# Choosing the experts by pairs of token tiles, and three rows of a hand-written schedule changed

## The reference

```python
xn = layernorm(x)
# of the encoder layer
s    = sigmoid(einsum('bsd,hed->bhse', xn, Wsel))      # for values and for output
gate = s * (one of the two largest of 8, else 0)
v    = einsum('bsd,bhse,hedp->bhsp', xn, gate_v, Wv)
o    = softmax(rope(q) @ rope(k) / 8) @ v
src2 = einsum('bhsp,bhse,hepd->bsd', o, gate_o, Wo)
h    = LN(xn + src2);  ffn = LN(h + relu(h @ W1 + b1) @ W2 + b2)
out  = x + causal_attention(xn) + ffn
```

## Time and profile before

| | |
|---|---|
| median of 3 runs | 3388.97 us (3387.23 to 3390.75) |
| profiled execution | 3392.11 us, span 3390.0 us |
| PE, PEld busy | 3202.1 us (94%), 2398.4 us (71%) |
| DVE, ACT, POOL busy | 2454.9 us (72%), 2006.9 us (59%), 1574.4 us (46%) |
| granted clock of TensorE | 0.992 in the mean |
| DMA | 295.26 MB, mean 87 GB/s |

### The profile page before, as it was taken

How to read it: one execution, slowest core, us unless ns; L and a number is a source line. 1 busy time by engine, 2 the same in 40 slices (tenths; PEclk the granted TensorE clock), 3 DMA queues, 4 the chain that set the end, 5 groups by cost and what they waited for, 6 DMA issues and landing times.

```text
span 3390.0 us, 67613 instructions
## 1 busy us (share of the span) xinstructions
PE 3202.1 (94%) x19648; PEld 2398.4 (71%) x19648; DVE 2454.9 (72%) x4716; ACT 2006.9 (59%) x4637; POOL 1574.4 (46%) x1295
## 2 busy tenths in 40 slices
PE   1699999999999999999999999999999999997997
PEld 1577777777777777777777777777777777775886
DVE  6577777777777777777777777777777777775776
ACT  2456666666666666666666666666666666664443
POOL 4143355445444454335533554435544544445666
PEclk9899999999999999999999999999999999998999
DMA  5233333233333332333332332333323423324122
GB/s 165 68 80 87 86 97 87 66 87 97 89 84 80 90 100 71 85 85 98 84 82 74 101 96 70 87 92 94 84 73 79 110 76 85 87 60 127 63 81 75
DMA packets 116487, 295.26 MB, mean 87 GB/s; under 512 B 33888, under 2 KB 54624, under 8 KB 100064
## 3 DMA queue, kind: packets, MB, share of 16 engines
q1 hardware_dynamic: 116448, 294.78, 33.3%
HBM read 262.74 MB, written 31.98 MB: 87 GB/s over the span
## 4 chain that ended last, share of the span: by engine, by line
PE 71%; DVE 19%; issue 6%; ACT 1%; DMA 1%; POOL 1%; DVEq 0%; SPq 0%; POOLq 0%; ACTq 0%
PE bank L710 24%; PE bank L837 14%; PE bank L755 9%; PE bank L811 7%; PE bank L725 5%; DVE nmax L1208 4%; PE bank L782 2%; DVE vm L1229 2%; PE bank L730 2%; PE bank L823 2%; PE bank L953 2%; DVE vm L1272 2%; DVE uf L1311 2%; PE bank L791 2%; DVE vm L1254 1%
## 5 line engine op out<-in xcount | busy, mean ns | idle before, releaser
L579 POOL TENSOR_TENSOR u_l<-uf,u_h 128x512 fp32r<-128x512 f32 x512 | 688.9, 1356 | 717.5 <-ACT u_h L1101 717.4
L1208 DVE TENSOR_REDUCE nmax<-bank 128x1 f32<-128x512 f32 (+3 forms) x1024 | 552.8, 581 | 375.4 <-PE bank L725 369.5
L710 PE MATMUL bank<-wv_h,xx 128*128 128x512 f32 x2048 | 744.8, 410 | 12.0 <-DVE vm L1229 7.1
L1017 ACT ACTIVATE probs<-bank,nmax 128x512 f32<-128x512 f32 (+3 forms) x1024 | 591.4, 610 | 259.1 <-DVE nmax L1208 259.1
L1101 ACT ACTIVATE u_h<-uf 128x512 fp32r<-128x512 f32 x512 | 323.0, 631 | 657.4 <-DVE uf L1311 498.7
L710 PEld LDWEIGHTS bank<-wv_h,xx 128*128 128x128 f32 x2048 | 386.6, 189 | 193.1 <-issue 69.3
L575 POOL TENSOR_TENSOR v_sb<-v_next,zero_hb 128x512 f32<-128x512 f32 x64 | 74.6, 1166 | 893.8 <-PE bank L811 879.2
L837 PE MATMUL bank<-u_h,wo_h 128*128 128x512 f32 x1024 | 433.4, 423 | 34.3 <-issue 27.5
L755 PE MATMUL bank<-ident_sb,probs 128*128 128x128 f32 x3328 | 451.8, 274 | 2.3 <-ACT pt_e L1037 1.2
L755 PEld LDWEIGHTS bank<-ident_sb,probs 128*128 128x128 f32 x3328 | 387.4, 141 | 69.1 <-issue 13.5
L1311 DVE TENSOR_TENSOR uf<-oo,go 128x512 f32<-128x512 f32 x512 | 426.6, 843 | 10.1 <-POOL u_l L579 7.9
(11 more groups left out here) (167 smaller groups left out, 5595.5 us busy)
## 6 DMA issues: line engine op xcount, KB each, us to landing
go<-go_d SPq DMA_DIRECT2D x256, 512.0 KB, 6.6
xx<-xs_d SPq DMA_DIRECT2D x128, 512.0 KB, 5.0
oo<-scale_d SPq DMA_DIRECT2D x128, 128.0 KB, 2.9
a_d<-a_out SPq DMA_DIRECT2D x128, 128.0 KB, 2.3
pt_c<-in_x SPq DMA_DIRECT2D x16, 512.0 KB, 4.7
st<-in_wv SPq DMA_DIRECT2D x16, 512.0 KB, 5.8
st<-in_wo SPq DMA_DIRECT2D x16, 512.0 KB, 7.8
go_d<-go_turned SPq DMA_DIRECT2D x256, 8.0 KB
```

What stands on the lines that cost most here:

```text
L579: nc.gpsimd.tensor_tensor(u_l[:, e % 2], uf[:, e % 2], u_h.bitcast(f32)[:, e % 2], ALU.subtract).then_inc(ul_done, 1)
L710: last = nc.tensor.matmul(out, lhs, rhs, start=n == 1, stop=n == 3 * len(chunks))
L1017: nc.scalar.activation(probs[:, s % 2, j, 0:w], sbank[j][:, 0:w], ACT.Exp, bias=nmax[:, 2 * s + j:2 * s + j + 1], **kw).then_inc(exp_done, 1)
L1208: nc.vector.tensor_reduce(nmax[:, 2 * s + j:2 * s + j + 1], sbank[j][:, 0:w], AX.X, ALU.max, negate=True).then_inc(nmax_ready, 1)
```

## The change

The choice is made for two token tiles at a time instead of four: CH has four jobs (pair, half) instead of two, each of the same steps on tensors half as wide, with the transposition at the end of pair 1 alone. `level`, `one`, `two` and `odds` get buffers of their own; EX is two jobs, each behind its two evictions. In the tables, pair 0 (CH0, CH1) stands in row 0 of DVE, CH2 in row 2 and CH3 in row 3; gates V0 and V1 move to row 1, gate V4 to row 4 and V6 to row 6; U6 moves from row 4 to row 5; on PE, V3 and J3 change places.

```diff
-           [("V", 2), ("J", 2), ("V", 3)],
-           [("J", 3), ("J", 4), ("V", 4)],
+           [("V", 2), ("J", 2), ("J", 3)],
+           [("V", 3), ("J", 4), ("V", 4)],
...
-ACT_FILL = [[("P", 0), ("P", 1), ("P", 2), ("P", 3), ("EX", 0), ("UH", 0), ("AC", 0), ("UH", 1)],
+ACT_FILL = [[("P", 0), ("P", 1), ("EX", 0), ("P", 2), ("P", 3), ("EX", 1), ("UH", 0), ("AC", 0), ("UH", 1)],
...
-DVE_FILL = [[("CH", 0), ("ON", 0), ("U", 0), ("U", 1)],
-            [("CH", 1)],
-            [("U", 2), ("V", 0), ("U", 3)],
-            [("V", 1), ("U", 4), ("V", 2), ("U", 5)],
-            [("V", 3), ("U", 6)],
-            [("V", 4), ("QL", 0), ("QL", 1), ("U", 7)],
-            [("V", 5), ("RECIP", 0)],
-            [("V", 6), ("V", 7), ("YA", 0)]]
+DVE_FILL = [[("CH", 0), ("CH", 1), ("ON", 0), ("U", 0), ("U", 1)],
+            [("V", 0), ("U", 2), ("V", 1)],
+            [("U", 3), ("CH", 2)],
+            [("U", 4), ("V", 2), ("U", 5), ("CH", 3)],
+            [("V", 3), ("V", 4)],
+            [("U", 6), ("QL", 0), ("QL", 1), ("U", 7)],
+            [("V", 5), ("RECIP", 0), ("V", 6)],
+            [("V", 7), ("YA", 0)]]
...
+        odds = sb("odds", [NP, TT, NG])
+        level, one, two = (sb(name, [NP, TT // 2, NG]) for name in ("level", "one", "two"))
...
-                        if kind != PRO:
-                            act.wait_ge(v_ready, 8 * n)
-                        nc.scalar.activation(odds, raw[:, :, NQK + NA:], ACT.Exp, scale=-1.0).then_inc(odds_ready, 1)
+                        nc.scalar.activation(odds[:, ts], raw[:, ts, NQK + NA:], ACT.Exp, scale=-1.0).then_inc(odds_ready, 1)
...
-                def choose(half):
+                def choose(pair, half):
...
+                    ts = slice(2 * pair, 2 * pair + 2)
...
-                        step(nc.vector.tensor_scalar(level, raw[:, :, NQK + NA:], SIG_ONE, None, ALU.min))
+                        step(nc.vector.tensor_scalar(level[:], raw[:, ts, NQK + NA:], SIG_ONE, None, ALU.min))
...
-                        step(nc.vector.tensor_scalar(odds, odds, 1.0, None, ALU.add))
+                        step(nc.vector.tensor_scalar(odds[:, ts], odds[:, ts], 1.0, None, ALU.add))
```

More of the change, by code:

```diff
@@ L206, in build @@
         rstd = sb("rstd", [NP, TT])
-        best = sb("best", [NP, TT * 4])
+        best = sb("best", [NP, TT // 2 * 4])
+        odds = sb("odds", [NP, TT, NG])
+        level, one, two = (sb(name, [NP, TT // 2, NG]) for name in ("level", "one", "two"))
         rest = rot[:, 0].rearrange("q t g c -> q g t c")
@@ L221, in build @@
         x_low = [(q_l[:], k_l[:]), (u_l[:, 0], u_l[:, 1])]
-        level, one, two, odds = (vm[:, i // 2, i % 2 * (S // 2):i % 2 * (S // 2) + TT * NG].rearrange("q (t n) -> q t n", t=TT) for i in range(4))
         hidden_f = [pe8[:, i] for i in range(4)]
@@ L1053, in do @@
                     elif name == "EX":
-                        for t in range(TT):
+                        ts = slice(2 * i, 2 * i + 2)
+                        for t in (2 * i, 2 * i + 1):
                             at, prior, _ = w_at(kind, it, ("P", t))
                             act.wait_ge(w_free[at], prior + 1)
-                        if kind != PRO:
-                            act.wait_ge(v_ready, 8 * n)
-                        nc.scalar.activation(odds, raw[:, :, NQK + NA:], ACT.Exp, scale=-1.0).then_inc(odds_ready, 1)
+                        nc.scalar.activation(odds[:, ts], raw[:, ts, NQK + NA:], ACT.Exp, scale=-1.0).then_inc(odds_ready, 1)
                     elif name == "PA":
@@ L1198, in _ @@
                 norm_in(b)
-            CHOOSE = 17
+            CHOOSE = 2 * 17 - 1
             n_c = 0
@@ L1231, in v_gate @@
                     nc.vector.tensor_reduce(v_next[:, t, j, :], m, AX.X, ALU.add).then_inc(v_ready, 1)
-                def choose(half):
+                def choose(pair, half):
                     nonlocal n_c
-                    n_c = half * CHOOSE // 2
+                    n_c = pair * (CHOOSE // 2) + half * 8
                     def step(ins):
@@ L1246, in groups @@
                         return ap.rearrange("q t (g e) -> q t g e", e=E)
-                    top = best[:].rearrange("q (t g) -> q t g", t=TT)
-                    top_b = top.unsqueeze(3).to_broadcast([NP, TT, 4, E])
-                    rank_b = rank_sb[:, None, None, :].to_broadcast([NP, TT, 4, E])
+                    ts = slice(2 * pair, 2 * pair + 2)
+                    top = best[:].rearrange("q (t g) -> q t g", t=TT // 2)
+                    top_b = top.unsqueeze(3).to_broadcast([NP, TT // 2, 4, E])
@@ L1252, in first_best @@
+                    rank_b = rank_sb[:, None, None, :].to_broadcast([NP, TT // 2, 4, E])
                     def first_best(dst):
[L1253 to L1256, removed]
@@ L1257, in first_best @@
-                        step(nc.vector.tensor_tensor(groups(dst), groups(dst), top_b, ALU.is_equal))
+                        step(nc.vector.tensor_reduce(top, groups(level[:]), AX.X, ALU.max))
+                        step(nc.vector.tensor_tensor(groups(dst[:]), groups(level[:]), top_b, ALU.is_equal))
+                        step(nc.vector.tensor_tensor(groups(dst[:]), groups(dst[:]), rank_b, ALU.mult))
+                        step(nc.vector.tensor_reduce(top, groups(dst[:]), AX.X, ALU.max))
@@ L1259, in choose @@
+                        step(nc.vector.tensor_tensor(groups(dst[:]), groups(dst[:]), top_b, ALU.is_equal))
                     if half == 0:
-                        for t in (TT - 2, TT - 1):
+                        for t in (2 * pair, 2 * pair + 1):
                             at, prior, _ = w_at(kind, it, ("P", t))
                             dve.wait_ge(w_free[at], prior + 1)
-                        step(nc.vector.tensor_scalar(level, raw[:, :, NQK + NA:], SIG_ONE, None, ALU.min))
+                        step(nc.vector.tensor_scalar(level[:], raw[:, ts, NQK + NA:], SIG_ONE, None, ALU.min))
@@ L1264, in choose @@
                         first_best(one)
-                        step(nc.vector.scalar_tensor_tensor(level, one, -BIG, level, ALU.mult, ALU.add))
-                        dve.wait_ge(odds_ready, n + 1)
-                        step(nc.vector.tensor_scalar(odds, odds, 1.0, None, ALU.add))
-                        assert n_c == CHOOSE // 2, n_c
+                        step(nc.vector.scalar_tensor_tensor(level[:], one[:], -BIG, level[:], ALU.mult, ALU.add))
+                        dve.wait_ge(odds_ready, 2 * n + pair + 1)
@@ L1269, in choose @@
+                        step(nc.vector.tensor_scalar(odds[:, ts], odds[:, ts], 1.0, None, ALU.add))
                         return
                     first_best(two)
[L1271 to L1278, removed]
+                    step(nc.vector.tensor_tensor(one[:], one[:], two[:], ALU.add))
+                    step(nc.vector.reciprocal(odds[:, ts], odds[:, ts]))
+                    step(nc.vector.tensor_tensor(gv[:, ts].rearrange("q t j e -> q t (j e)"), odds[:, ts, 0:2 * E], one[:, :, 0:2 * E], ALU.mult))
@@ L1280, in do @@
+                    last = nc.vector.tensor_tensor(go_rows[:].rearrange("q (t n) -> q t n", t=TT)[:, ts], odds[:, ts, 2 * E:], one[:, :, 2 * E:], ALU.mult)
+                    if pair == 1:
+                        step(last)
+                        if kind != PRO:
+                            dve.wait_ge(go_stored, 64 * n)
+                        nc.vector.transpose(go_turned[:], go_rows[:]).then_inc(go_ready, 1)
+                    assert n_c == (CHOOSE // 2, CHOOSE)[pair], n_c
                 def do(job):
@@ L1284, in do @@
                     elif name == "CH":
-                        choose(i)
+                        choose(i // 2, i % 2)
                     elif name == "QL":
```

## The result

The changed kernel takes 3862.38 us in the median of 4 runs (3844.91 to 3875.49), the kernel before 3389.86 us in 4 runs: a ratio of 1.1387, 95% interval 1.1335 to 1.1438. The forecast was slower, 3745 us, with a range up to 3840. Direction and mechanism were right, the size was too small by 117 us. The profiled execution took 3844.91 us (span 3842.9), at a mean granted clock of 0.945, where before it was 0.992.

What follows compares the result with a forecast made beforehand. PE was taken to bound the kernel, 46.54 us a round. V5 later by 5.45 us plus 0.25 for the clock made 5.7 x 62 = 353, plus 2 for the last round: 3745 us, range 3610 to 3840.

Steps and rivals of the forecast that it cites:

- Pair 0 costs nothing: DVE, row 0: pair 0 starts about 2.1 us earlier and the 4.42 us gap covers it; uncovered it would cost 4.7.
- Two-operand steps wait for POOL: DVE's CH2 and CH3: each two-SBUF-operand step waits for the running POOL instruction, with waits of 0.21 to 0.99 us.
- The open point: CH2's last step, TENSOR_SCALAR on `odds`: no row showed whether it waits for POOL; assumed 0.35 us, otherwise 22 us less.
- CH2 starts 17.1 after P0, S6 32.24, by the later layout 32.84: DVE's pair 1 beside POOL: CH2 starts near 1629.5, delaying row maxima 5 and so scores S6 by 1.7 us.
- the later layout: Alternative order on DVE and POOL: UL2 gets ahead of CH2's third step, and the layout ends 0.6 us later.
- From S6 to V5 8.3 us: U6 behind row maxima 6 holds up UH6 and ACT's list: 8.3 us instead of 4.6, V5 5.45 us later.
- From V5 to P0 nothing changes: End of the round on PE, from V5 to the next P0: stays at 11.4 us.
- The clock, 0.25 a round with ends 0 and 0.9: TensorE may sometimes fall to half clock behind waits of 2.0 to 2.5 us: 0.25 us a round, between 0 and 0.9.
- PE falls to half clock in every round: Rival, chance 0.07: S6 0.9 and one product after V5 1.4 us longer, 7.75 a round, 3870 us.
- The rival without contention: POOL does not hold up DVE's short steps; only U6's chain is left, 2.1 us a round, 3520 us; chance 0.10.
- The rival in which the waits at J4 and V3 come back as a gain: PE's bank waits go and U6's chain is covered: 0.9 us a round back, 3333 us; chance 0.03.

Runs made afterwards that it cites:

- the fill: The changed kernel with transposes T4 made four times, T5 twice and QK1 five times in PE's waits, results unchanged: 3785.36 us.
- U6 back: The changed kernel with U6 back in row 4 of DVE's table and gate V4 in row 5: 3630.11 us.
- UH6 away: The changed kernel with U6 left late and UH6 moved behind QH1 in ACT's table: 3659.33 us.
- the first new table: The kernel before, choice unsplit, DVE's table changed: U2 and U3 ahead of V0, U4 to U6 ahead of V3, RECIP behind V6: 3427.77 us.
- the split alone: The kernel before with the choice split in pairs with own buffers, both where the halves stood, gates, U6 and expert products in old order: 3497.73 us.

## Why the prediction was right in kind and too small

Step by step, with times after P0 where that is plainer:

- *Pair 0 costs nothing*: right. DVE's gap of 4.42 us is 2.25, and pair 0 ends 7.7 us after P0 (forecast 7.6), before the attention product.
- *Two-operand steps wait for POOL*: right, and shown from both sides, by changing DVE's operands (324 us back) and POOL's lengths (254 back). The open point, whether TENSOR_SCALAR waits too, is settled: the one on `odds` takes 1.10 beside UL3 and 195 ns when UL is short. The Trainium skill, "SBUF — State Buffer", Who interferes with whom, says that tensor_scalar can contend with GpSimd and that tensor_reduce on trn2 never does; the rows agree on both.
- *CH2 starts 17.1 after P0, S6 32.24, by the later layout 32.84*: CH2 started at 17.14, and S6 at 32.87. UL2 began at 1689.62, 0.12 us ahead of the step on `rank_sb` (in the listed order CH2's fourth, where the prediction says third). This fits the layout that I had called a matter of 0.1 us and did not take. CH2 ended 1.1 us later than laid out, 21.77 after P0, and U4, laid out with a wait of 0.5, had none. The net is the smaller miss, 0.6 us a round.
- *From S6 to V5 8.3 us*: 8.37. The terms as listed end at 1652.8 and not at 1653.0, 0.17 us less; from row maxima 6 (1706.61) to V5 (1713.10) 6.49 were measured, which is the 6.5 used and not the 6.33 listed. T5's wait (2.0) was 1.95 where PE came to T5 at full clock and at most 0.6 elsewhere, V5's (0.6) came in 32 of 62 rounds, S7's (1.0) was 0.2 to 0.8; UH6 waited 3.84 (about 4). That it is ACT's list which carries this was shown by moving UH6 alone.
- *From V5 to P0 nothing changes*: right at full clock, 11.38 us (1553.70 to 1565.08) against 11.41. In the round shown it takes 13.20, the first 3.8 of them at half clock; that is the price of the next term.
- *The clock, 0.25 a round with ends 0 and 0.9*: this is the step that failed. I sized it by one wait of 2.2 us behind which the clock fell, as something that "may" happen "sometimes", while the change makes PE wait 2.9 us at S6 and up to 2.0 at T5 within 9 us, and again in each round. Measured: half clock in 61 of 61 rounds, which costs 1.85 us in 36 of them and nothing in 25. That is 1.09 us a round, and 1.07 to 1.24 by the fill: four to five times the term.

By the profiled execution the round grew by 7.2 us, not 5.7: 0.65 of the difference is the layout (V5 comes 6.1 later, not 5.45) and about 0.85 the clock. 62 x 1.5 = 93, and 3745 + 93 = 3838, against the 3844.91 of that execution; the median of the four runs lies 17 higher still; the other three have mean clocks of 0.942 to 0.944, this one 0.945. The upper end of the forecast's own range, 6.95 a round and 3820, had both terms together, the layout at 0.6 and the clock at 0.9, and is the nearest by its terms. The rival "PE falls to half clock in every round", at a chance of 0.07, is what happened, but its 3870 us lie near the 3862 by luck: it put 2.3 us a round on the clock, twice what was measured, and left the later layout out. Against it I had held that waits of 0.44 us don't do it, which says nothing of waits of 3 us; the rows that could speak spoke for it. The Trainium skill, "TensorE: Matmul & The Clock Gate", HAM oscillation, tells of a kernel whose recurring wait makes each round start cold; this trace agrees in that the fall recurs in 61 of 61 rounds, though here it lies late in the round, from 32 us after P0 on, and not at its start.

The rival without contention (3520) was tested by itself: with one-operand steps 3537.9. The rival in which the waits at J4 and V3 come back as a gain (3333) needed U6's chain covered and the contention gone: with both 3350.31.

## What to carry to other kernels

Look, before moving short dependent steps on DVE into a gap, at what POOL does there: each two-operand step can pay for the rest of a whole POOL instruction, and a chain of eighteen steps pays several times. An instruction that waits at the head of an in-order list charges its wait to everything behind it, so when a producer moves, its first reader should move with it, and the same holds for DMA queues (RECIP and the load of x). When a change brings waits of PE that recur each round, look in the trace for stretches at half clock behind waits as long, put them into the sum as a case and not as a mishap, see whether a later wait of PE covers them, and look for harmless work that could fill the waits.

## What the runs showed of the hardware

- Adding transposes to PE made the kernel 77 us faster, since the clock stayed at 1.00 (0.993 in the mean, 0.945 without them).
- Half clock costs nothing where a later wait of PE takes it up: 25 rounds of the change have it ahead of T5 and last 52.67 us, 36 behind T5 and last 54.52. With U6 back 43 of 61 rounds have it and last 50.50 in the mean, the other 18 last 50.21.
- How often the clock fell went with the waits of a round, full rounds of 61 with a stretch at 0.5: all with waits of 2.9, up to 2.0, up to 0.8 and 0.6 (the change), 43 with one of 2.9 (U6 back), 42 likewise (UH6 away), 42 with 1.7, 0.8 and 0.6 (short instructions on POOL), 44 with 1.1, 0.8, 0.5 and 0.4 (U6 late in the kernel before), 20 with 1.1, 0.8 and 0.6 (one-operand steps), 13 with one of 1.5 in the mean (the first new table), none with 1.0, 0.5 and 0.4 (the split alone). Why rounds with like waits differ, no run here tells.
